# Attention of one layer on one core: bursts of four score pairs with one whole key tile of values behind each, instead of bursts of three with parts of tiles

## The reference, cut to what matters

```python
x = L0_attn_x                                   # (1, 1024, 512)
xn = _layernorm(x)
# attention: EMBED = 512, H = 32, KV = 8, D = 16, REP = H // KV = 4
xq, xk, xv = xn @ wq + bq, xn @ wk + bk, xn @ wv + bv
q, k = _rope(xq, cos, sin), _rope(xk, cos, sin)
scores = einsum('bqhd,bkhd->bhqk', q, repeat(k, REP)) / sqrt(D)
s = einsum('bhqk,bkhd->bqhd', softmax(scores), repeat(v, REP))
# gate: z = xn W^T + b; m = low-rank experts; gamma from the two norms
g = silu(z + gamma * m)
return x + s * g
```

## Time and profile before

| | |
|---|---|
| median of 3 runs | 434.01 us |
| profiled execution, its own time | 434.95 us |
| its span | 433.1 us |
| PE busy, share of the span | 421.8 us, 97% |
| VectorE (DVE) busy | 370.9 us, 86% |
| ScalarE (ACT) busy | 309.9 us, 72% |
| GpSimd (POOL) busy | 139.3 us, 32% |
| granted TensorE clock, mean | 0.988 |

### The profile page before, as it was taken

How to read it: one execution, slowest core, us unless ns; L and a number is a source line. 1 busy time by engine, 2 the same in 40 slices (tenths; PEclk the granted TensorE clock), 3 DMA queues, 4 the chain that set the end, 5 groups by cost and what they waited for, 6 DMA issues and landing times.

```text
span 433.1 us, 8295 instructions
## 1 busy us (share of the span) xinstructions
PE 421.8 (97%) x3153; PEld 182.5 (42%) x3153; DVE 370.9 (86%) x613; ACT 309.9 (72%) x612; POOL 139.3 (32%) x195
## 2 busy tenths in 40 slices
PE   8989999998999999999999999999999999999994
PEld 3647433343344444444444344444444344433331
DVE  5844798998799999999999999999999999923443
ACT  2231011237689898998989998999999998867774
POOL 7872323345002230403143040305123230401555
PEclk9999999998699999999999999999999999999999
DMA  8949995444000020000000000000000000011002
GB/s 260 306 110 126 134 126 73 73 76 73 4 0 3 2 58 3 0 4 2 4 0 3 2 3 5 2 2 2 3 2 4 0 3 4 3 48 40 21 23 67
DMA packets 13624, 18.09 MB, mean 42 GB/s; under 512 B 3168, under 2 KB 7552, under 8 KB 13584
## 3 DMA queue, kind: packets, MB, share of 16 engines
q1 hardware_dynamic: 12064, 16.44, 20.1%
q10 hardware_dynamic: 1520, 1.12, 1.0%
HBM read 6.72 MB, written 2.10 MB: 20 GB/s over the span
## 4 chain that ended last, share of the span: by engine, by line
PE 87%; POOL 3%; DVE 3%; ACT 2%; DMA 2%; issue 2%; SPq 1%; DVEq 0%; POOLq 0%; ACTq 0%
PE st L1122 32%; PE oT L1090 27%; PE st L934 6%; PE sm L1199 3%; PE oT L1175 3%; PE oT L934 3%; PE sm L1038 2%; PE sm L1013 2%; PE sm L1099 2%; DMA x_sb<-in_x 2%; PE st L1154 2%; PE st L963 2%; DVE negmax L795 1%; POOL arena L466 1%; PE sm L1205 1%
## 5 line engine op out<-in xcount | busy, mean ns | idle before, releaser
L803 DVE TENSOR_REDUCE neghalf<-sm 128x1 f32<-128x512 f32 x448 | 270.9, 679 | 3.2 <-PE sm L1013 2.9
L709 ACT ACTIVATE arena<-st 128x512 f32<-128x512 f32 x448 | 232.9, 599 | 22.9 <-PE st L1122 18.1
L1013 PE MATMUL sm<-kA,qA 48*128 48x512 f32 x448 | 158.7, 447 | 0.0
L1122 PE MATMUL st<-qA,kA 50*128 50x512 f32 x448 | 156.0, 444 | 1.5 <-DVE z_sb L846 1.1
L1090 PE MATMUL oT<-arena,vg 128*32 128x256 f32 (+3 forms) x1568 | 130.7, 425 | 0.0
L1122 PEld LDWEIGHTS st<-qA,kA 50*128 50x128 f32 x448 | 74.4, 186 | 99.6 <-ACT arena L709 82.8
L537 POOL TENSOR_TENSOR rsum<-junk,consts 128x16 f32<-128x16 f32 x13 | 37.9, 2916 | 128.0 <-ACT junk L681 128.0
L1013 PEld LDWEIGHTS sm<-kA,qA 48*128 48x128 f32 x448 | 74.5, 186 | 2.8 <-DVE neghalf L803 2.3
L1090 PEld LDWEIGHTS oT<-arena,vg 128*32 128x32 f32 x1568 | 33.7, 109 | 47.1 <-issue 41.6
L795 DVE TENSOR_REDUCE negmax<-sm 128x1 f32<-128x1024 f32 x32 | 37.9, 1217 | 7.0 <-PE sm L1038 7.0
L730 ACT ACTIVATE arena<-st 128x512 f32<-128x512 f32 x48 | 26.9, 601 | 12.6 <-PE st L1154 12.6
(11 more groups left out here) (122 smaller groups left out, 361.9 us busy)
## 6 DMA issues: line engine op xcount, KB each, us to landing
qA<-arena SPq DMA_DIRECT2D x45, 128.0 KB, 5.1
x_sb<-in_x SPq DMA_DIRECT2D x8, 256.0 KB, 6.0
kA<-qA SPq DMA_DIRECT2D x12, 128.0 KB, 6.7
wT_sb<-in_wT SPq DMA_DIRECT2D x1, 1024.0 KB, 7.5
out<-x_sb SPq DMA_DIRECT2D x1, 896.0 KB, 4.1
out<-x_sb SPq DMA_DIRECT2D x4, 224.0 KB, 1.9
z_sb<-in_wq SPq DMA_DIRECT2D x1, 768.0 KB, 10.4
qA<-qA SPq DMA_DIRECT2D x3, 128.0 KB, 3.8
```

What stands on the lines that cost most here:

```text
L709: act.activation(probs[:, s % PB, h, :], st[:, st_score(0, s, h) % 3, :], ACT.Exp, scale=float(D) ** -0.5).then_inc(st_free, 1)
L803: dve.tensor_reduce(neghalf[:, e // 16, e % 16, j % 2:j % 2 + 1], sm[:, n % 4, :], AX.X, ALU.max, negate=True).then_inc(sm_free, count)
L1013: pe.matmul(sm[:, n % 4, :], qA[rows, half, g // 2, h, qt * P:(qt + 1) * P], kA[rows, g // 2, kh * HALF:(kh + 1) * HALF], start=True, stop ...
L1122: pe.matmul(st[:, n % 3, :], kA[rows, g // 2, kt * P:(kt + 1) * P], qA[rows, half, g // 2, h, :], start=True, stop=True).then_inc(st_full, 1)
```

## The change

The burst becomes one key tile: four pairs, and behind it one block of values with the whole tile before it (LAG = 1), 512 columns wide. A half has 8 bursts and 8 blocks. `block_parts` and CUTS go. The three banks of `st` stay. The turned maxima stand before pairs 8 and 40, the turned heads before pairs 16 and 48, and `evacuate` behind the exponentials of (0, 3) and (8, 3). In the last group one block of group 6 is left over instead of two, and stands behind its first tile of scores.

```diff
-MAX1_AT, MAX0_AT = 9, 41
-OUT1_AT, OUT0_AT = 18, 50
-BURST, LAG = 3, 2
-BURSTS = -(-REP * NT // BURST)
-BLOCKS = 2 + 3 * (NT - 2) // 2
-CUTS = ((0, 0, 384), (0, 384, HALF), (1, 0, 256), (1, 256, HALF))
+MAX1_AT, MAX0_AT = 8, 40
+OUT1_AT, OUT0_AT = 16, 48
+LAG = 1
+BLOCKS = NT
...
 def blocks_through(g, s):
-    kt = s % NT
-    return 2 * BLOCKS * g + BLOCKS * (s // NT) + (1 + (3 * kt + 1) // 2 if kt < NT - 1 else BLOCKS)
+    return 2 * BLOCKS * g + s + 1
...
-                        if (s, h) == (1, 1) and not first:
+                        if (s, h) == (0, 3) and not first:
                             evacuate(blocks_through(g - 1, 2 * NT - 1), 1, (sm_full, sm_out1(g - 1) + 1))
-                        if (s, h) == (9, 1):
+                        if (s, h) == (8, 3):
                             evacuate(blocks_through(g, NT - 1), 0, None if first else (sm_full, sm_out0(g - 1) + 1))
...
             def values(g, half, b):
-                s = NT * half + block_parts(b)[-1][0]
-                pe.wait_ge(st_free, st_score(g, s, 3) + 1)
+                pe.wait_ge(st_free, st_score(g, NT * half + b, 3) + 1)
...
-                for kt, first_col, end_col in block_parts(b):
-                    cols = slice(first_col, end_col)
-                    for h in range(REP):
-                        mm = pe.matmul(oT[h * VC:(h + 1) * VC, cols], vg[:, g % 2, kt, :],
-                                       probs[:, (NT * half + kt) % PB, h, cols],
-                                       start=(kt == 0), stop=(kt == NT - 1))
+                for h in range(REP):
+                    mm = pe.matmul(oT[h * VC:(h + 1) * VC, :], vg[:, g % 2, b, :], probs[:, (NT * half + b) % PB, h, :],
+                                   start=(b == 0), stop=(b == NT - 1))
                 mm.then_inc(pv_done, 1)
...
-                    half, kt, burst = s // NT, s % NT, i % (REP * NT) // BURST
+                    half, kt, burst = s // NT, s % NT, s % NT
...
-                    if i % (REP * NT) % BURST != BURST - 1 and i % (REP * NT) != REP * NT - 1:
+                    if h != REP - 1:
                         continue
...
                     if u == 0:
-                        values(LAST - 1, 1, BLOCKS - 2)
+                        values(LAST - 1, 1, BLOCKS - 1)
...
                     last_scores(2 * u + 1)
-                    if u == 0:
-                        values(LAST - 1, 1, BLOCKS - 1)
-                    elif u < NT - 1:
+                    if 0 < u < NT - 1:
                         last_block(2 * u - 2, 2 * u - 1)
```

More of the change, by code:

```diff
@@ L85 @@
 ST_PER, SM_PER = 66, 66
-MAX1_AT, MAX0_AT = 9, 41
-OUT1_AT, OUT0_AT = 18, 50
-BURST, LAG = 3, 2
-BURSTS = -(-REP * NT // BURST)
-BLOCKS = 2 + 3 * (NT - 2) // 2
-CUTS = ((0, 0, 384), (0, 384, HALF), (1, 0, 256), (1, 256, HALF))
-assert BLOCKS == BURSTS
+MAX1_AT, MAX0_AT = 8, 40
+OUT1_AT, OUT0_AT = 16, 48
+LAG = 1
+BLOCKS = NT
 def st_score(g, s, h):
```

## The result

The changed kernel took 465.62 us (median of 5 runs, 464.0 to 469.17), the kernel before 433.45 us beside it. The ratio is 1.0747 (95% interval 1.0713 to 1.0781), so it is slower by about 32 us. The profiled execution took 469.17 us, 3.5 us over the median, with a span of 467.3 us.

What follows compares the result with a forecast made beforehand. VectorE was taken to bound the kernel (19.41 us a half), the ring to replace it; 25.1 us for groups 1 to 6, 3 for group 0 and 0.4 for the last sum to 28.5, giving 462.5 us, range 452 to 471.

Steps and rivals of the forecast that it cites:

- The ring: In each burst, first score, its exponential, fourth load, values and block form a wait loop of 2.59 us, over VectorE's 2.42.
- What comes out from under cover: In each group, PE's other work, formerly hidden by VectorE's backlog, counts in full: 1.32 + 0.06 + 0.2 us.
- Turned heads: Two a group, each adding 0.66 us: 0.59 on PE and 0.07 from their copy on ScalarE.
- turned maxima: Two a group, where a block takes 1.03 us instead of 1.00; 0.06 us a group.
- evacuation: Copy of oT at the end of burst 0 delays the next burst's first exponential about 0.1 us, twice a group.
- The sum by stretches: Over the whole kernel: 25.1 us more in groups 1 to 6, 3 in group 0, 0.4 in the last group.
- the forecast's 0.4 us: Last group: one leftover block instead of two, the first standing before the second tile's scores; +0.4 us (-0.5 to +0.5).
- PE is close behind: Kernel before, groups 0 to 6: VectorE sets the pace at 19.41 us a half, with PE's work nearly as long.
- the ring's upper bound: In every burst, the 1.03 us block and 0.04 us more at the wait give at most 2.67 us.
- Rival (a): The fourth pair's wait is hidden and VectorE stays the bound: 432 to 434.5 us; chance 0.07.
- Rival (b): The fourth load or its values come sooner, a burst taking 2.47 to 2.50 us: 451 us; chance 0.08.
- Rival (c): PE's halt in every burst lowers the clock; a fifth of 112 bursts at the low level gives 494 us; chance 0.04.

Runs made afterwards that it cites:

- split kernel: Changed kernel with each burst's values block cut into two 256-column pieces, behind the third and fourth pairs; ratio to the kernel before 1.0343, about 449 us.
- the kernel with the smaller blocks: Changed kernel with values blocks of groups 0 to 6 over 256 columns, the other half left out; executions 439.38, 448.32, 462.85 and 507.77 us.

## Why the prediction was right

The forecast was 462.5 us in a range of 452 to 471; 465.6 was measured, 32 us more than before where 28.5 were forecast.

- **The ring.** Forecast 0.53 + 0.63 + 0.43 + 1.00 = 2.59 us. Found 0.53 + 0.65 + 0.43 + 1.00 = 2.61. Shown as the cause three ways: a shorter exponential helps only if it is the burst's first, VectorE's work does not matter, and the wait goes with the fourth pair moved.
- **What comes out from under cover.** Turned heads forecast 0.66, found 0.71 us (3.32 - 2.61); turned maxima 0.03, found 0.04; evacuation 0.1, found 0.10. A group is 2 x 21.73 = 43.46 us against the 43.02 forecast: 16 x 0.02 = 0.32 from the ring and 0.1 from the turned heads.
- **The sum by stretches.** From one profiled execution to the other the span grew by 34.2 us, by the first scores of each stretch: 4.2 up to group 1 (145.30 to 149.46), where 3 were forecast; 27.8 in groups 1 to 6 (232.90 to 260.71), where 25.1 were; and 2.2 in the last group (54.9 to 57.1), where 0.4 were. In this last stretch the clock was at 0.50 for 3.4 us, as it was not before (0.96 in the mean behind the last copy of turned maxima, 1.00 before). From that copy to the end the two executions took 49.7 and 47.9 us. In the kernel with the second exponential cut, which has the changed kernel's last group and where the clock held 1.00 until PE's work was all but over, it was 48.1 us, so most of the 1.8 us is the clock and the forecast's 0.4 us is borne out. In group 0 the clock was at 0.50 for 13.7 us, 10.2 before. Two blocks with the turned maxima between them were 4.16 us apart there (106.75 to 110.91), forecast at some 4.
- **What was wrong, though it did not show in the sum.** I read PE as having some 17.7 us of work in a half of the changed kernel, and for the kernel before I said that "PE is close behind" and, in the expectations, took 18.8 to 18.9 us. With VectorE's work cut, that kernel still needed 19.30 us a half, since its third scores wait too: ScalarE's exponentials run back to back behind PE's bursts. The slack that I summed up from unhindered bursts is not there. The split kernel missed for a like reason: a single pair between two pieces costs 0.43 us, and I took the 0.34 of a pair that follows another. Two small slips: the terms of the ring's upper bound add up to 2.66 us and not 2.67, and a tile's exponentials end at about T + 2.6 (201.39 + 2.06 in the burst above), not T + 2.0, which is still 1.6 us ahead of the block that needs them.
- **Rival (a)** is out (halves of 21.7 us, VectorE idle). **Rival (b)**, a ring of 2.47 to 2.50 us, is out too. **Rival (c)**, the clock, did not come in the steady halves of the changed kernel (1.00), though it halts in each burst. The low level can last far longer than I reckoned with, though: see the last section.

Of the versions that leave nothing out (the split, LAG = 2), none beats the kernel before. More banks for the transposed scores weren't tried, since all eight are taken (four for the row scores, three, and oT).

## What to carry to other kernels

A ring of n banks stands for n tiles in flight between two engines. If a burst has n + 1 and little stands between its tiles, as here, the last one waits for the whole way there and back (here 0.53 + 0.65 us), and what stands behind it on the in-order engine is added to the period; busy shares of all engines then fall together. Before making bursts longer, compare burst and ring, and sum the way there and back with what stands in the queue, against the pace of the bound. And a slack summed up from unhindered durations should be tested by adding work to that engine: here 0.5 us a half by the sum was 0.07 us by the test.

## What the runs showed of the hardware that I had not expected

In the kernel with the smaller blocks the clock fell at the start of group 0, behind a stretch in which PE had 1.21 us of work in 2.30 us:

```profile
100.00:102.30 2.30, 1.21 (x8) 0.54 (x6) 1.62 (x3) 1.17 (x4) 1.01 (x3) 1.00 0.76 179
```

It then stayed at the low level (1.2 GHz) for 276 us, although PE shows as busy for 60.00 of 60.00 us in the stretch above, and came back at about 382 us with no change in the work; the next halves ran at the full level with PE busy for 18.87 of 19.34 us. In the changed kernel the same fall lasted 13.7 us, in the kernel before 10.2. The order of PE's work does not settle how long: the split kernel was at the low level for 41.0 us in its profiled execution, and for 6.8 us with the same order and the row maxima halved. Nor did each such halt bring a fall. With the first exponential and the maxima cut, about the same halt stands at the start of group 0, and the clock stayed at 1.00 up to the last group. Its row up to 102 us and the one behind:

```profile
100.00:102.00 2.00, 0.91 (x4) 0.11 (x3) 1.78 (x3) 0.87 (x4) 1.20 (x4) 1.00 0.62 170
...
104.00:120.00 16.00, 15.98 (x110) 5.69 (x111) 12.20 (x33) 13.72 (x32) 1.41 (x5) 1.00 0.11 14
```

With one profile of each kernel, what ends the low level stays open. For a reader of profiles it means that some microseconds between two kernels can be the clock's alone: compare their stretches at one level.

The Trainium skill (TensorE: Matmul & The Clock Gate, "A second HAM failure mode: psum-queue depth-cycling") tells of a clock that swings between the levels where a kernel cycles through PSUM banks with small gaps. The trace agrees in part: the clock had only two levels here, 0.50 and 1.00. But it did not swing in the ring: the changed kernel, with a halt of 0.24 us in each burst, held 1.00 for some 300 us, and the kernel with the smaller blocks had one long stay at the low level.
